# Adding layer 3's rows to the output by accumulating transfers from GpSimd instead of an add in SBUF

## The reference, cut to what matters

```python
h = jnp.maximum(_layernorm(x, axis=-1), 0.0)
x = x + _L3_gnn_ref(h, adj, L3_gnn_W)

def _L3_gnn_ref(x, adj, W):
    deg = jnp.sum(adj, axis=-1, keepdims=True)
    agg = jnp.einsum('bij,bjf->bif', adj, x) / jnp.maximum(deg, EPS)
    cat = jnp.concatenate([x, agg], axis=2)
    return jax.nn.relu(jnp.einsum('bnf,of->bno', cat, W))
```

## Time and profile before

| what | value |
|---|---|
| median of 3 runs | 2645.71 us (2644.42 to 2645.93) |
| the profiled execution's own time | 2646.03 us |
| its span | 2644.2 us |
| TensorE busy | 2602.5 us, 98% |
| VectorE, ScalarE, GpSimd busy | 70%, 53%, 55% |
| transfers | 196.03 MB, 21.6% of 16 engines on SyncE's queue |

### The profile page before, as it was taken

How to read it: one execution, slowest core, us unless ns; L and a number is a source line. 1 busy time by engine, 2 the same in 40 slices (tenths; PEclk the granted TensorE clock), 3 DMA queues, 4 the chain that set the end, 5 groups by cost and what they waited for, 6 DMA issues and landing times.

```text
span 2644.2 us, 44994 instructions
## 1 busy us (share of the span) xinstructions
PE 2602.5 (98%) x12962; PEld 2175.5 (82%) x12962; DVE 1847.2 (70%) x4104; ACT 1405.2 (53%) x2621; POOL 1455.1 (55%) x2276
## 2 busy tenths in 40 slices
PE   7999999999999999999999999999999999999999
PEld 5888888888888888888888888888888887788887
DVE  7777777777777767565656567676767666677776
ACT  4444344444444455454545455666666665666665
POOL 5444444444444655333333334777776767877776
PEclk9999999999999999999999999999999999999999
DMA  4111111111111221111111113232222223444443
GB/s 136 43 39 43 46 34 42 34 46 44 38 38 38 90 78 61 60 42 60 42 60 42 60 42 94 76 100 73 86 88 88 85 79 112 129 148 151 148 137 120
DMA packets 145816, 196.03 MB, mean 74 GB/s; under 512 B 55521, under 2 KB 55521, under 8 KB 145761
## 3 DMA queue, kind: packets, MB, share of 16 engines
q1 hardware_dynamic: 140288, 185.40, 21.6%
q10 hardware_dynamic: 5472, 9.96, 1.2%
HBM read 128.20 MB, written 67.11 MB: 74 GB/s over the span
## 4 chain that ended last, share of the span: by engine, by line
PE 93%; DVE 2%; ACT 1%; issue 1%; POOL 1%; DMA 1%; ACTq 0%; SPq 0%; POOLq 0%; DVEq 0%
PE ps L554 27%; PE ps L556 27%; PE ps L555 26%; PE ps L571 6%; PE ps L596 4%; PE ps L574 2%; ACT row_hi L810 0%; DVE row_lo L1062 0%; ACTq L829 0%; PE ps L738 0%; ACT w_hi L810 0%; POOL w_lo L1402 0%; PE ps L731 0%; DMA raw<-w_t 0%; PE ps L792 0%
## 5 line engine op out<-in xcount | busy, mean ns | idle before, releaser
L554 PE MATMUL ps<-w_hi,col_hi 128*128 128x512 f32 x2432 | 968.9, 398 | 5.0 <-DVE col_lo L1062 3.3
L556 PE MATMUL ps<-w_hi,col_lo 128*128 128x512 f32 x2432 | 949.7, 391 | 0.0
L555 PE MATMUL ps<-w_lo,col_hi 128*128 128x512 f32 x2432 | 947.9, 390 | 0.0
L554 PEld LDWEIGHTS ps<-w_hi,col_hi 128*128 128x128 f32 x2432 | 456.9, 188 | 98.6 <-DVE col_lo L1062 7.9
L556 PEld LDWEIGHTS ps<-w_hi,col_lo 128*128 128x128 f32 x2432 | 456.8, 188 | 98.8
L555 PEld LDWEIGHTS ps<-w_lo,col_hi 128*128 128x128 f32 x2432 | 458.0, 188 | 87.7 <-issue 0.2
L810 ACT ACTIVATE col_hi<-ps 128x512 fp32r<-128x512 f32 (+1 forms) x512 | 293.7, 580 | 269.3 <-PE ps L574 147.4
L1402 POOL TENSOR_TENSOR row_lo<-normed,row_hi 128x512 fp32r<-128x512 f32 x160 | 207.9, 1308 | 203.4 <-ACT row_hi L810 203.4
L1419 POOL TENSOR_TENSOR var_eps<-moments,eps_ln 128x1 f32<-128x1 f32 x256 | 55.5, 217 | 459.8 <-DVE moments L1079 431.8
L1062 DVE TENSOR_TENSOR col_lo<-ps,col_hi 128x512 fp32r<-128x512 f32 (+1 forms) x256 | 164.4, 648 | 135.7 <-ACT col_hi L810 135.7
L571 PE MATMUL ps<-adj_both,row_hi 128*128 128x256 f32 x1024 | 249.6, 329 | 6.1 <-DVE deg L1117 5.5
(11 more groups left out here) (157 smaller groups left out, 4788.6 us busy)
## 6 DMA issues: line engine op xcount, KB each, us to landing
out<-x_res SPq DMA_DIRECT2D x256, 256.0 KB, 2.0
x_in<-out SPq DMA_DIRECT2D x192, 256.0 KB, 2.8
x_res<-out SPq DMA_DIRECT2D x128, 256.0 KB, 3.2
x_in<-x SPq DMA_DIRECT2D x64, 256.0 KB, 2.6
adj_in<-adj_t SPq DMA_DIRECT2D x96, 64.0 KB, 2.4
raw<-wk ACTq DMA_DIRECT2D x14, 256.0 KB, 3.6
raw<-w ACTq DMA_DIRECT2D x12, 256.0 KB, 2.8
raw<-w_t ACTq DMA_DIRECT2D x10, 256.0 KB, 4.7
```

Of the source, the lines that this page charges most:

```text
L554: nc.tensor.matmul(out_ap, lhs_hi, rhs_hi, start=start, stop=False, **checks)
L555: nc.tensor.matmul(out_ap, lhs_hi, rhs_lo, start=False, stop=False, **checks)
L556: return nc.tensor.matmul(out_ap, lhs_lo, rhs_hi, start=False, stop=stop, **checks)
```

## The change

In layer 3, `x_res` is no longer used. The residual is already in `out`, in the rows that the store would write, so GpSimd's part of `fin` issues a transfer from c12 or c22 to those rows with an add as its operation. SyncE's four residual loads and four stores of each layer 3 group are left out. The next group's `p6` copy waits until both transfers of its pair have landed (`x_added`), and so does the end of the program. Layers 0 to 2 are as before.

```diff
+        x_added = [sem(f"x_added{t}") for t in range(SLOTS)]
@@ SyncE, body
-                if layer >= 2:
+                if layer == 2:
                     for t in range(SLOTS):
                         load_residual(layer, g, t)
-                for t in range(SLOTS):
-                    store_x(layer, g, t)
+                if layer < 3:
+                    for t in range(SLOTS):
+                        store_x(layer, g, t)
@@ SyncE, end
-                sp.wait_ge(x_stored[t], 16 * 4 * GROUPS)
+                sp.wait_ge(x_added[t], 16 * GROUPS)
@@ ScalarE, p6
-                    act.wait_ge(s["final"], nl(layer, g, b) - SLOTS)
+                    if layer == 3 and not first(g):
+                        act.wait_ge(x_added[a], 16 * g)
+                        act.wait_ge(x_added[b], 16 * g)
+                    else:
+                        act.wait_ge(s["final"], nl(layer, g, b) - SLOTS)
@@ GpSimd, mean, fin
-                    pool.wait_ge(xres_loaded[t], 16 * g + 16 * GROUPS + 16)
+                    pool.wait_ge(x_stored[t], 16 * 3 * GROUPS)
                     at = c22_at(t // 2) if t % 2 else c12_at(t // 2)
-                    Q.tensor_tensor(x_res[:, t, :], x_res[:, t, :], at, ALU.add).then_inc(s["final"], 1)
+                    pool.dma_start(out_tiles[bass.ds(g * SLOTS + t, 1)].rearrange("n p f -> p (n f)"), at,
+                                   accum_op=ALU.add).then_inc(x_added[t], 16)
```

## The result

| | before | after |
|---|---|---|
| median, 18 runs each | 2645.89 us (2644.26 to 2648.13) | 2650.61 us (2648.16 to 2652.51) |
| ratio, 95% interval | | 1.0016, 1.001 to 1.0022 |
| the profiled execution | 2646.03 us, span 2644.2 | 2649.15 us, span 2647.5 |

The change makes the kernel 4.7 us slower (2.6 to 5.8 by the interval). The median is under the 0.2% called "no change" and inside the range of 2644.4 to 2655. But the interval leaves out zero, so 18 runs of each do tell it from none, the time is 4 us above the forecast of 2646.6, and the loss has one place, the end of the program.

A forecast was written before the change was run, and what follows sets the result against it. TensorE alone was taken to bound layer 3's loop, with only the end different. With 0 in the loop and +0.84 us at the end, the median of 2645.71 gave 2646.6 us, called no change; range 2644.4 to 2655.

The forecast's parts named there:

- What bounds the kernel: Layer 3's loop: TensorE alone sets the 23.68 us a group; work taken off GpSimd or SyncE gains nothing.
- The issue on GpSimd: `fin` in layer 3: each of 64 issues takes 1.25 us, like the add it replaces; cost 0.
- the bound of 2.5 us: GpSimd in layer 3's loop: each issue may take about 2.5 us before TensorE stops.
- Landing: ScalarE's p6 copy waits for transfers landing 4.1 us after issue start; TensorE stops only above about 7.2 us; cost 0.
- The end: End of program: 4.1 us from the last `fin`'s start to landing replaces 3.26 us to the store's landing, +0.84 us.
- Rival 1: Layer 3's p6 copy: landing passes 7.2 us and holds up p7 in groups 1 to 15; 2669 us, chance 0.13.
- Rival 2: GpSimd in layer 3: issues over 2.5 us make TensorE wait for `row_lo`; 2671 us at 3.0 us, chance 0.07.
- Rival 3: SyncE runs ahead and transfers calm down: a real gain, over 5.3 us, chance 0.04.

The follow-up runs named there:

- e5: The changed kernel with each adding transfer cut into two of 128x256: 2649.20 us beside 2645.86 for the kernel before, ratio 1.0012.
- e6: The changed kernel with each adding transfer cut into four of 128x128: 2731.16 us beside 2645.86 for the kernel before, ratio 1.0321.
- e4: The changed kernel with plain transfers instead of adding ones, so old rows are overwritten: 2648.70 us beside 2646.43 for the kernel before, ratio 1.0008.
- e7: The changed kernel with GpSimd's issue for slot 1 moved behind the next group's `w_lo` pair: 2653.14 us beside 2645.86 for the kernel before.
- e8: The changed kernel with GpSimd's issue for slot 1 moved behind slot 3's: 2758.78 us beside 2645.86 for the kernel before, ratio 1.0425.
- e12: The kernel before with adding transfers in layer 3's groups 0 to 14, last group's clip and add joined on VectorE: 2645.92 us beside 2646.93.
- e1: The changed kernel with layer 3's group 15 added and stored the old way: 2648.52 us beside 2646.43 for the kernel before, ratio 1.0008.

## Why the prediction was right, and where not

**What bounds the kernel: right.** Taking 1.4 us of GpSimd's work and SyncE's 14 us waits away from each group moved the period by nothing.

**The issue on GpSimd (its time D, 1.25 us taken): too long.** It is 0.88 us, and GpSimd's next pass starts 0.6 us after its start (2565.28 and 2565.92). Nothing hung on it, since the bound of 2.5 us was never near; e5 and e6 have that bound between 1.8 and 3.5.

**Landing (L = 4.1 us taken): right in the loop.** The two kinds have medians of 4.0 and 4.8 us, slot 1's own lands 3.9 to 4.2 us after its issue in the groups looked at. That it fits so well is partly luck: of the sum 3.2 + 0.9, the 0.9 for a longer issue is 0.88 - 0.34 = 0.5 by measurement, and that the write streams behind the read, so that 3.2 us cover both, was the author's assumption. No run shows the read and the write of an adding transfer apart; what the runs show is the whole, 4.0 to 4.8 us. The last one of the program takes 4.9, 0.8 us more than taken, which is the smaller part of the miss at the end (1.6 - 0.84 = 0.8 of 3.2 us). The recorded traffic didn't stay equal either: the pages have 111.43 MB read instead of 128.20 and 67.11 MB written in both, and 16.78 MB on GpSimd's queue with adding as without (e4), so the pages count no read of the old rows. The transfer engines' share in the window of a group went from 0.44 to 0.49.

**The end (+0.84 us): this term failed.** The step read "3.26 us from the start of the last `fin` ... Now it is L from the same start". It took for granted that the program closes a fixed time after the last landing (0.45 us before the change). It closes when GpSimd's drain is over, 2.66 us after the landing. The term measured +4.0: 1.6 for the landing and 2.4 for the drain. With it the sum is 2645.7 + 4.0 = 2649.7, where 2650.6 was measured. That the measured time still lies in the range is luck: the upper end was made for a landing of 7.5 us that stops TensorE, which didn't happen, and not for a longer close.

**Rival 1** has the right place, and e7 and e8 show its bound; its price was too low, since a landing in a row of three takes longer (6.2 us in e8 instead of 4.8), and since TensorE's work behind the stop ran at a granted clock of 0.5 for 3.8 us. **Rival 2** likewise: the place is right (`row_lo`, `w_lo`), the waits were 3.0 us a group where 3.1 had been worked out, but the group grew by 4.75 (e6). **Rival 3**, a gain, isn't there.

## What to carry to other kernels

Handing an add to a transfer can pay only if the engine that did the add is on the path; here TensorE was full (23.70 of 23.70 us), and the 1.4 us of GpSimd's work that it freed a group was worth nothing. Cost the end of a program with every engine's closing drain. GpSimd's took about 0.08 us for each 256 KB transfer it had issued (for 1 to 64 of them), and with 64 fresh adding ones it ended 2.6 us after the last landing. Let GpSimd's list end early, as in e12, where 5 us of drain cost nothing; giving only the transfers of the last group back to SyncE, as in e1, leaves the drain at the end. A wait that moves from an instruction to a landing should be checked by its room, from the issue to the waiter, and priced with what a stopped TensorE loses in clock behind it (2.0 us a group in e8, 1.7 in e6).

## What the runs showed that was not expected

- GpSimd's closing drain grows with the number of transfers it issued: 0.17, 0.75 and 5.0 us for 1, 8 and 60. In e5 with 128 smaller ones it ended 4.16 us after the last issue, 0.8 after the last landing, and in e6 with 256 it ended 4.0 and 2.0 us after them. So the line does not go on; why is open.
- An adding 256 KB transfer to memory takes 4.0 to 4.8 us to land against 2.3 to 2.5 for a plain one from the same queue, and 2.8 times the transfer engines' time (4.5% to 1.6%).
- Stops of 5 us a group took another 2 us a group through the lowered clock in e8.
